# Flamingo block with two ternary and 8-bit-quantised products: the weights' magnitudes are summed in the first phase and their signs are taken by ScalarE

## The chip, the cores and the metric

The kernel runs on 1 core of one Trainium2 chip. The metric is the device time of one execution in microseconds (us), as the median of several runs. Engines: PE is TensorE (PEld its weight loads), DVE is VectorE, ACT is ScalarE, POOL is GpSimd, SP is SyncE, which here only issues DMAs.

## The reference

Inputs are `x` and a context, both 16 x 256 x 512 in float32, with weights. The result is `x` after four residual steps, each scaled by the tanh of a gate:

1. `x += tanh(g) * attention(layernorm(x), ctx)` with 16 heads, projections Wq, Wk, Wv, Wo and a strided mask;
2. `x += tanh(g) * experts(layernorm(x))`, where every expert picks one token of each group of 16 by a maximum of logits;
3. `x += tanh(g) * attention(layernorm(x), ctx)` without projections, with a mask;
4. `x += tanh(g) * ffn(layernorm(x))`, with

```
h   = layernorm(x) * ln_g + ln_b
h   = quant8(h) @ ternary(w1).T          w1: 2048 x 512
h   = gelu(h)                            exact
out = quant8(h) @ ternary(w2).T          w2: 512 x 2048

quant8(a):  amax = max(quantile(|a|, 0.995), 1e-5);  clip(round(a*127/amax), -128, 127)*amax/127
ternary(w): gamma = mean(|w|) + 1e-5;  clip(round(w/gamma), -1, 1)*gamma
```

So a ternary weight is gamma times -1, 0 or +1, and it is not 0 where |w| is over gamma/2. The kernel keeps the -1, 0 and +1 as bf16, transposed (`w1T`, `w2T`), and multiplies gamma in later.

## The kernel before

The program is a row of stages, each a block in which the five engines run their own instruction lists and meet at semaphores; a barrier of all engines ends a stage.

**phase1** (line 157) does residual step 1 and the logits of step 2. It works one batch entry (256 tokens) at a time, as a software pipeline of 18 steps: step b does F for entry b (turning the context and the normalised x by TensorE transposes, the k, v and q projections), M for entry b-1 (scores, softmax, attention, output projection) and T for entry b-2 (second layernorm, logits, selections). Steps 2 to 13 run as a loop of pairs, the others are written out; F, M and T are absent where there is no entry. Each engine's list of a step is written by hand in the function `step` of its block. What matters at the end of a step: TensorE does the output projection of entry b-1 into two PSUM banks (`rows_of("o", ...)`, line 344), VectorE adds each bank to the residual (line 791, semaphore `x1_done`), SyncE waits for `x1_done` and issues the write of that entry (line 316). SyncE's next step begins with the loads of x and ctx for the next entry (lines 278, 283). ScalarE's list of a step ends with a wait for TensorE's output projection and no work. What matters at the start of a step: TensorE turns the context of entry b (line 328), ScalarE copies it from PSUM as the high part `p_ctxTh` (line 503), VectorE subtracts to get the low part `p_ctxTl` (line 646), TensorE does the scores of entry b-1 (lines 378 to 387) and then turns the normalised x into the same two PSUM banks as the context, so it waits for `p_ctxTl` before it does.

**phase2a** and **phase2b3** do the experts and residual step 3, and leave the layernormed rows `hid` and the candidates `cand` (the 8 largest magnitudes of each stretch) for the first quantile.

**quantile1** (line 1675) finds the 0.995 quantile in 16 rounds of a radix-four search on the bits. In a round VectorE makes four trial values (line 1810), VectorE counts `cand` against two of them (line 1813), ScalarE against one (a Relu at 1744 and a Sign at 1746), TensorE sums the counts over the partitions (1763, the tile `q_tot`), and VectorE picks (1820, 1822). Beside it the ternary w1 is made: SyncE loads w1 and w2 whole (1706, 4 MB each); ScalarE sums magnitudes by an Abs with an accumulator, 2048 columns at a time, four for w1 in rounds 1 to 4 and four for w2 in rounds 6 to 9 (line 1726); gamma and the thresholds plus and minus gamma/2 (`th`, `nth`) come from line 1730 on; POOL compares each 128 x 2048 piece of w1 with `nth` and with `th` (1715, 1716), which gives two masks in bf16; TensorE turns both masks into one PSUM bank, the one by the identity and the other by minus the identity, so that the bank holds above minus below (`ternary_turn`, 1568); ScalarE evicts each bank of 128 x 512 into `w1T` (1739), two banks a round in rounds 8 to 15.

**quantise_hidden** and **product_tops** quantise `hid`, multiply by `w1T`, apply Gelu, and leave candidates again.

**quantile2** (line 2000) searches the second quantile in 17 rounds over whole numbers. In a round VectorE makes one trial (1620, 2097), ScalarE maps it by Gelu (2073) and counts 2304 columns of `cand` by a Sign (2075), VectorE counts the other 1792 (2100), TensorE sums (2053, 2055), VectorE decides (1624, 1627). Beside it `w2T` is made in the same way as `w1T`, a quarter of w2 at a time: SyncE loads 1 MB (2027), POOL makes two masks (2035, 2036), TensorE turns four banks, and ScalarE evicts them (2069), two at the end of each of two rounds.

**ffn** multiplies by `w2T` and adds to the output.

```
def phase1 ... def step(b, par, F, M, T, L):      # SyncE, the end of a step
    if M:
        sp.wait_ge(s["x1_done"], n.next(s["x1_done"], NT))
        n.apart()
        sp.dma_start(xm[b - 1], x1[1 - par][:, :, :]).then_inc(s["x1_out"], 16)
def phase1 ... def step(b, par, F, M, T, L):      # ScalarE, the start and the end
    if F:
        for t in range(NT):
            high(ctxT, t, "ctx_high")
    ...
    if M:
        act.wait_ge(s["M_full"], n.next(s["M_full"], NT))
```

Of the kernel before, what the change touches and what calls it, by code (L numbers as in the profile page):

```python
# [156 lines left out]
def phase1(nc, x, ctx, gx, Wq, bq, Wk, bk, Wv, bv, Wo, bo, ctrl, K, x_mid, xparts, perm_d, vg_d):  # L157
# [5 lines left out]
    with ExitStack() as es:  # L163
# [333 lines left out]
        def _(act):  # L497
# [1177 lines left out]
def quantile1(nc, cand, hid, K, amax, w1, w2, w1T, gam, th, nth):  # L1675
# [3 lines left out]
    ABS = {0: (1, 2, 3, 4), 1: (6, 7, 8, 9)}  # L1679
    SUM = {4: 0, 9: 1}  # L1680
    GAMMA = {5: 0, 10: 1}
    TURN = {8 + k: (2 * k, 2 * k + 1) for k in range(WQ * GQ // 2)}
    with ExitStack() as es:
        sw = es.enter_context(semaphores(nc, "qa_", [f"{q}_{n}" for q in ("q1", "q1s") for n in Search.NAMES] + """w_in0 w_in1 quads_in trial_ready
            above_done act_counted counted4 told4 step4 consts identb_done summed sums_full tsum_done gamma_done th_done signs_done turn_full turn_taken""".split()))
# [6 lines left out]
        W = [sbt(f"w{k}", [P, FC * D]) for k in range(2)]  # L1692
        sink, asum, tsum, eps = sbt("sink", [P, WC], BF16), sbt("asum", [P, 2 * WQ]), sbt("tsum", [P, 2]), sbt("eps", [P, 1])
        below_w, over_w = [[sbt(f"{n}{i}", [P, WC], BF16) for i in range(2)] for n in ("below", "above")]
        identb, minus = sbt("identb", [P, P], BF16), sbt("minus", [P, P], BF16)
# [5 lines left out]
        @block.sync  # L1701
        def _(sp):
            sp.dma_start(quads[:, :], K["c_quads"]).then_inc(sw["quads_in"], 16)
            fast.load(sp)
            for k, (w, rows) in enumerate(((w1, FC), (w2, C))):
                sp.dma_start(W[k][:, :].rearrange("p (c k) -> p c k", c=rows), w.rearrange("(c p) k -> p c k", p=P)).then_inc(sw[f"w_in{k}"], 16)
            slow.load(sp)

        @block.gpsimd
        def _(pool):  # L1710
            pool.wait_ge(sw["th_done"], 1)
            for k in range(WQ):
                if k >= 2:
                    pool.wait_ge(sw["turn_full"], GQ * (k - 1))
                pool.tensor_scalar(below_w[k % 2][:, :], W[0][:, k * WC:(k + 1) * WC], nth[:, 0:1], None, ALU.is_lt)
                pool.tensor_scalar(over_w[k % 2][:, :], W[0][:, k * WC:(k + 1) * WC], th[:, 0:1], None, ALU.is_gt).then_inc(sw["signs_done"], 1)

        @block.scalar
        def _(act):

# [16 lines left out]
            def turned(g):  # L1737
                act.wait_ge(sw["turn_full"], g + 1)
                act.activation(w1T[:, :, g * P:(g + 1) * P], bturn[g % 2][:, :].rearrange("p (c k) -> p c k", c=C), ACT.Copy).then_inc(sw["turn_taken"], 1)

            act.wait_ge(sw["consts"], 1)
            for r in range(ROUNDS):
# [5 lines left out]
                for w in range(2):  # L1748
                    if r in ABS[w]:
                        absolute(w, ABS[w].index(r))  # L1750
                if r in GAMMA:
                    thresholds(GAMMA[r])
                for g in TURN.get(r, ()):
                    turned(g)

        @block.tensor
        def _(pe):
            n = Count(pe)
            pe.wait_ge(sw["consts"], 1)
            for r in range(ROUNDS):  # L1760
# [3 lines left out]
                if r in SUM:  # L1764
                    w = SUM[r]
                    pe.wait_ge(sw["summed"], (w + 1) * WQ)
                    pe.matmul(bsum[:, w * WQ:(w + 1) * WQ], fast.ones[:, :], asum[:, w * WQ:(w + 1) * WQ], start=True, stop=True).then_inc(sw["sums_full"], 1)
# [694 lines left out]
```

## Time and profile before

| | us |
|---|---|
| median of 3 runs | 1668.54 (1667.11 to 1671.72) |
| the profiled execution, its own time | 1669.37 |
| its span in the trace | 1667.6 |
| TensorE busy | 1328.3 (80%) |
| VectorE busy | 1022.5 (61%) |
| ScalarE busy | 743.1 (45%) |
| POOL busy | 507.4 (30%) |

The span is 1.8 us shorter than the profiled execution's time, which has the launch around it. phase1 takes about the first third of the span, the first search runs from 1169.5 to 1252.3 us and the second from 1433.7 to 1533.4 us. In phase1 TensorE has nearly no idle time; in the two searches every engine has some, and a round is as long as the chain of waits from one trial to the next.

### The profile page before, as it was taken

Reading aid. Unit: us, or ns where it says so; the run is one execution under the profiler, and the core shown is the slowest. Engines: PE = TensorE matmul, PEld = TensorE weight load, DVE = VectorE, ACT = ScalarE, POOL = GpSimd, SP = SyncE. Lnnn points to the kernel's source line nnn. Section 1 sums busy time; section 2 is a strip of 40 time slices with the busy share of each in tenths; the row PEclk is TensorE's granted clock in tenths of the full one; section 3 lists DMA queues with packets and bytes.
Section 4 is the critical chain, followed back from the end, with each engine's and each line's share of the span. In section 5 each row is a group of like instructions: output and inputs, shape, how many; then the busy total and the mean of one; then the engine's idle time right before and its main releaser. Section 6 shows DMA issues by size and latency. Waiting matters only on the chain. (4 is left out here: it accounts for less than half of the span.)

```text
span 1667.6 us, 24905 instructions
## 1 busy us (share of the span) xinstructions
PE 1328.3 (80%) x8908; PEld 935.9 (56%) x8930; DVE 1022.5 (61%) x2344; ACT 743.1 (45%) x1113; POOL 507.4 (30%) x435
## 2 busy tenths in 40 slices
PE   5999999999999639999948999983143899133996
PEld 5887888788878437666415666653133444132443
DVE  5576667766675423444425878775566488745774
ACT  3233333333333113344414565552774555355991
POOL 1133333333333110000004787865180000253011
PEclk9999999999999769999979999996555899555998
DMA  6112221212211175565789788830500477211974
GB/s 212 46 65 72 85 100 66 70 69 101 80 65 46 65 271 193 224 244 216 276 275 287 235 233 232 236 96 25 207 1 3 173 305 304 77 47 35 413 311 154
DMA packets 105207, 259.18 MB, mean 155 GB/s; under 512 B 17456, under 2 KB 28816, under 8 KB 97424
## 3 DMA queue, kind: packets, MB, share of 16 engines
q1 hardware_dynamic: 95808, 232.59, 40.0%
q0 software_dynamic: 6384, 24.12, 3.9%
q10 hardware_dynamic: 2912, 1.14, 0.3%
q8 instruction: 59, 0.97, 0.3%
q14 instruction: 44, 0.36, 0.1%
HBM read 152.18 MB, written 105.64 MB: 155 GB/s over the span
## 5 line engine op out<-in xcount | busy, mean ns | idle before, releaser
L1191 PE MATMUL p_s<-p_rows,p_permT 128*128 128x512 f32 x256 | 132.0, 614 | 1.1 <-ACT p_permT L1284 1.1
L913 PEld LDWEIGHTS p_sel<-p_pick,p_xp 128*128 128x128 bf16 x1536 | 89.2, 100 | 57.5 <-issue 31.1
L913 PE MATMUL p_sel<-p_pick,p_xp 128*128 128x128 bf16 x1536 | 100.7, 223 | 23.8 <-DMA p_xp<-xparts 22.7
L2296 PE MATMUL p_o<-w2T,p_Gq 128*128 128x512 bf16 x501 | 111.7, 383 | 8.4 <-DVE p_Gq L2353 7.9
L1937 PE MATMUL p_z<-qT,w1T 128*128 128x512 bf16 x501 | 112.6, 385 | 3.0 <-PEq L113 2.5
L1043 DVE COPY p_selT<-p_sel 128x512 f32<-128x512 f32 x64 | 44.3, 692 | 99.8 <-PE p_sel L913 99.8
L2035 POOL TENSOR_SCALAR q_wbelow<-q_w,nth 128x2048 bf16<-128x2048 f32 x4 | 21.8, 5442 | 228.2 <-DMA q_w<-in_L_ffn_w_dram 192.6
L1996 DVE MAX8 cand<-hid 128x8 f32<-128x128 f32 x384 | 74.7, 296 | 25.3 <-ACT hid L1984 25.3
L2296 PEld LDWEIGHTS p_o<-w2T,p_Gq 128*128 128x128 bf16 x512 | 50.3, 99 | 69.4 <-DVE p_Gq L2353 8.1
L1937 PEld LDWEIGHTS p_z<-qT,w1T 128*128 128x128 bf16 x512 | 50.6, 99 | 64.8 <-issue 6.0
L990 ACT ACTIVATE p_selT<-p_sel 128x512 f32<-128x512 f32 x64 | 38.2, 598 | 91.8 <-PE p_sel L913 91.8
L344 PE MATMUL p_M<-p_ctxTh,p_Wkh 128*128 128x256 f32 x256 | 75.4, 295 | 1.9 <-DVE p_Wkl L668 1.9
L344 PE MATMUL p_M<-p_xnTh,p_Wqh 128*128 128x256 f32 x256 | 75.0, 293 | 1.1 <-DVE p_V L741 1.1
L2053 PE MATMUL q_tot<-q_signs,q_half 128*128 128x1 f32 x34 | 9.9, 362 | 79.3 <-ACT q_junk_a L2075 79.3
L344 PE MATMUL p_M<-p_ctxTh,p_Wkl 128*128 128x256 f32 x256 | 72.7, 284 | 0.0
L344 PE MATMUL p_M<-p_ctxTl,p_Wkh 128*128 128x256 f32 x256 | 72.7, 284 | 0.0
L344 PE MATMUL p_M<-p_xnTl,p_Wqh 128*128 128x256 f32 x256 | 72.0, 281 | 0.0
L344 PE MATMUL p_M<-p_xnTh,p_Wql 128*128 128x256 f32 x256 | 72.0, 281 | 0.0
L892 POOL DMA_DIRECT2D p_f<-in_L_ffn_f_dram x16 | 8.9, 556 | 201.0 <-PE p_in L930 195.2
L1763 PE MATMUL q_tot<-q_cnt,q_ones 128*128 128x4 f32 x32 | 9.3, 360 | 76.0 <-ACT q_junk_a L1746 40.2
L510 ACT ACTIVATE p_qT<-p_M,p_bqT 128x256 f32<-128x256 f32 x64 | 26.9, 471 | 95.4 <-PE p_M L344 95.4
L592 POOL TENSOR_TENSOR p_rs<-p_ve,p_mhalf 128x2 f32<-128x2 f32 x32 | 22.4, 699 | 154.0 <-DVE p_ve L658 153.9
(334 smaller groups left out, 4016.8 us busy)
## 6 DMA issues: line engine op xcount, KB each, us to landing
inter_d<-p_stage SPq DMA_DIRECT2D x64, 512.0 KB, 3.2
p_rows<-inter_d SPq DMA_DIRECT2D x128, 256.0 KB, 5.3
activations<-hid SPq DMA_DIRECT2D x24, 1024.0 KB, 3.9
p_cin<-in_ctx_dram SPq DMA_DIRECT2D x32, 512.0 KB, 5.1
xparts<-p_parts SPq DMA_DIRECT2D x16, 768.0 KB, 3.3
hid<-activations SPq DMA_DIRECT2D x10, 1024.0 KB, 8.9
p_xp<-xparts SPq DMA_DIRECT2D x3, 3072.0 KB, 25.2
p_xin<-in_x_dram SPq DMA_DIRECT2D x16, 512.0 KB, 4.1
```

What stands on the lines that cost most here:

```text
L344: mm = pe.matmul(out, left[a][:, c, lcols], right[e][:, c, rcols], start=(k == 0), stop=(k == len(terms) - 1))
L510: a = act.activation(dst[:, c, :], bM[k][:, (c % 2) * S:(c % 2 + 1) * S], ACT.Identity, bias=bias[:, c:c + 1])
L592: pool.tensor_tensor(out[:, :], var[:, :], mhalf[:, :], ALU.pow).then_inc(s[done], 1)
L913: mm = pe.matmul(bsel[u % 2][:, k * P:(k + 1) * P], xp[:, c, tile, r, :], pick[sb % 2][:, tile, :, :].rearrange("p s g -> p (s g)"), start ...
L990: act.activation(*picked(q, u), ACT.Copy).then_inc(s["sel_act"], 1)
L1043: dve.tensor_copy(*picked(q, u)).then_inc(s["sel_dve"], 1)
L1191: mm = pe.matmul(bo[t][:, :], permT[b % 2][:, t, k, :], R[b % 2][:, t, k, :], start=(k == 0), stop=(k == NK - 1))
L1937: mm = pe.matmul(bank, w1T[:, c, fc * P:(fc + 1) * P], qT[:, c, bass.ds(first, TB)], start=(c == 0), stop=(c == C - 1))
L1996: a = dve.max(cand[:, c:c + 8], Gs[j % R][:, :, k * OCT:(k + 1) * OCT])
L2035: pool.tensor_scalar(below_w[:, :], wc[:, :], nth[:, 1:2], None, ALU.is_lt)
L2053: pe.matmul(fast.tot[:, 0:1], half[:, :], signs[:, :], start=True, stop=False)
L2296: mm = pe.matmul(bo[i % 2][t][:, :], Gq[n % QR][:, k, t * P:(t + 1) * P], w2T[:, h * QUAD + k, :], start=(h == 0 and k == 0), stop=(h == N ...
```

## The change

The magnitudes of w1 and w2 are summed in phase1: in each of the 16 steps that have F, SyncE loads 256 KB of each matrix into `wabs` at the very end of its step, after the residual's write, and ScalarE takes an Abs with an accumulator of both at the very end of its step. `asum` (two tiles of 128 x 16) is carried to the first search, where the sums over partitions and both thresholds are made in round 0. w2 is no longer loaded in the first search.

POOL has no part in the searches any more. ScalarE takes two signs of each piece, sign(w - gamma/2) and sign(w + gamma/2), by a Sign with `nth` and with `th` as its bias: in the first search one in each of rounds 1 to 8, in the second in rounds 1, 2, 4, 5, 7, 8, 10 and 11. TensorE turns both by half the identity, so that a bank holds half the sum of the signs. VectorE evicts the banks in place of ScalarE, two in a round, between its count and its wait for TensorE's sum, and adds and subtracts MAGIC (3 * 2^22), which rounds to a whole number: rounds 4 to 11 of the first search, rounds 3, 4, 6, 7, 9, 10, 12 and 13 of the second.

```
@@ phase1 @@
+        wabs = sbt("wabs", [P, 2, D])
+        wv = [w.rearrange("a b -> (a b)").rearrange("(n p k) -> n p k", p=P, k=D) for w in (w1, w2)]
@@ phase1, SyncE, the end of step @@
                     sp.dma_start(xm[b - 1], x1[1 - par][:, :, :]).then_inc(s["x1_out"], 16)
+                if F:
+                    if (used := n.reuse(s["abs_done"])) is not None:
+                        sp.wait_ge(s["abs_done"], used)
+                        n.apart()
+                    for k in range(2):
+                        sp.dma_start(wabs[:, k, :], wv[k][b]).then_inc(s["abs_in"], 16)
@@ phase1, ScalarE, the end of step @@
                     act.wait_ge(s["M_full"], n.next(s["M_full"], NT))
+                if F:
+                    act.wait_ge(s["abs_in"], n.next(s["abs_in"], 32))
+                    for k in range(2):
+                        a = act.activation(wabs[:, k, :], wabs[:, k, :], ACT.Abs, accum_out=asum[k][:, bass.ds(b, 1)])
+                    a.then_inc(s["abs_done"], 1)
@@ ternary_turn @@
-        pe.matmul(bank[:, i * P:(i + 1) * P], over[:, cols], identb[:, :], start=True, stop=False)
-        mm = pe.matmul(bank[:, i * P:(i + 1) * P], below[:, cols], minus[:, :], start=False, stop=True)
+        for k in range(2):
+            mm = pe.matmul(bank[:, i * P:(i + 1) * P], signs[k][:, cols], halfid[:, :], start=(k == 0), stop=(k == 1))
@@ quantile1 @@
-    ABS = {0: (1, 2, 3, 4), 1: (6, 7, 8, 9)}
-    SUM = {4: 0, 9: 1}
-    GAMMA = {5: 0, 10: 1}
-    TURN = {8 + k: (2 * k, 2 * k + 1) for k in range(WQ * GQ // 2)}
+    SIGN = {1 + i: i for i in range(2 * WQ)}
+    TURN = {3 + 2 * k + i: (GQ * k + 2 * i, GQ * k + 2 * i + 1) for k in range(WQ) for i in range(2)}
...
-        def _(pool):
...
@@ quantile1, ScalarE @@
+            def sign(i):
+                c, k = divmod(i, 2)
+                if i == 0:
+                    act.wait_ge(sw["w_in"], 16)
+                    act.wait_ge(sw["th_done"], 2)
+                if c >= 2 and k == 0:
+                    act.wait_ge(sw["turn_full"], GQ * (c - 1))
+                act.activation(signs[c % 2][k][:, :], W[:, c * WC:(c + 1) * WC], ACT.Sign, bias=(nth, th)[k][:, 0:1]).then_inc(sw["signs_done"], 1)
...
+                if r == 0:
+                    act.wait_ge(sw["sums_full"], 1)
+                    for w in range(2):
+                        thresholds(w)
+                if r in SIGN:
+                    sign(SIGN[r])
@@ quantile1, VectorE, after the two counts of a round @@
+                for g in TURN.get(r - 1, ()):
+                    dve.wait_ge(sw["turn_full"], g + 1)
+                    dve.tensor_scalar(w1T[:, :, g * P:(g + 1) * P], bturn[g % 2][:, :].rearrange("p (c k) -> p c k", c=C), MAGIC, MAGIC, ALU.add, ALU.subtract).then_inc(sw["turn_taken"], 1)
@@ quantile2 @@
-    TURN = {4 + 3 * k + i: (GQ * k + 2 * i, GQ * k + 2 * i + 1) for k in range(WQ) for i in range(2)}
+    SIGN = {1 + 3 * c + k: (c, k) for c in range(WQ) for k in range(2)}
+    TURN = {2 + 3 * k + i: (GQ * k + 2 * i, GQ * k + 2 * i + 1) for k in range(WQ) for i in range(2)}
...
```

SyncE's list in phase1, from one step's end into the next step's start, inside the loop of pairs. `p_sharedk` holds the finished residual rows, `p_wabs` the new tile. Before:

```order
L316 ISA [waits p1_x1_done]
L316 DMA residual<-p_sharedk 128x2x512
L276 REGISTER_ALU [waits p1_norm1]
L278 ISA [waits p1_xb_done]
L278 DMA p_xin<-in_x_dram 128x2x512
L283 DMA p_cin<-in_ctx_dram 128x2x512 [waits p1_ctx_high]
```

and now:

```order
L318 ISA [waits p1_x1_done]
L318 DMA residual<-p_sharedk 128x2x512
L324 ISA [waits p1_abs_done]
L324 DMA p_wabs<-in_L_ffn_w_dram 128x512 x2
L278 REGISTER_ALU [waits p1_norm1]
L280 ISA [waits p1_xb_done]
L280 DMA p_xin<-in_x_dram 128x2x512
L285 DMA p_cin<-in_ctx_dram 128x2x512 [waits p1_ctx_high]
```

The two loads of a step stand behind the wait for `x1_done` of that step and ahead of the next step's loads.

ScalarE's list at the same place. Before:

```order
L579 ACTIVATE p_perm<-p_T 128x128 [waits p1_perm_out,p1_T_full]
L582 REGISTER_ALU
L502 REGISTER_ALU [waits p1_M_full]
L503 ACTIVATE p_ctxTh<-p_T 128x4x128 [waits p1_T_full]
L502 REGISTER_ALU
L503 ACTIVATE p_ctxTh<-p_T 128x4x128 [waits p1_T_full]
L528 REGISTER_ALU
L529 ACTIVATE p_sharedo<-p_S 128x512 [waits p1_S_full]
```

and now:

```order
L587 ACTIVATE p_perm<-p_T 128x128 [waits p1_perm_out,p1_T_full]
L590 REGISTER_ALU
L592 ISA [waits p1_M_full]
L594 ISA [waits p1_abs_in]
L594 ACTIVATE p_wabs,asum<-p_wabs 128x512
L594 REGISTER_ALU
L594 ACTIVATE p_wabs,asum<-p_wabs 128x512
L510 REGISTER_ALU
L511 ACTIVATE p_ctxTh<-p_T 128x4x128 [waits p1_T_full]
```

Between the wait for the output projection and the first copy of the next step there is now a wait for a DMA (`abs_in`) and two instructions.

VectorE's list in the first search, in a round from 4 to 11, now (before, the two rows of line 1817 were not there):

```order
L1807 TENSOR_TENSOR q_trial<-q_cur,q_quads 128x5 [waits p1_perm_done]
L1810 TENSOR_SCALAR q_junk,q_cnt<-cand,q_trial 128x1024 [waits p1_xnT]
L1810 TENSOR_SCALAR q_junk,q_cnt<-cand,q_trial 128x1024
L1817 TENSOR_SCALAR w1T<-q_turn 128x4x128 [waits p1_S_full] x2
L1819 SCALAR_TENSOR_TENSOR q_sel<-q_tot,q_trial 128x4 [waits p1_atT_global]
L1821 TENSOR_REDUCE q_cur<-q_sel 128x1 [waits p1_perm_done]
```

The two evictions stand ahead of the wait for TensorE's sum (semaphores are used again by later stages, so the names printed here are those of phase1).

## Rows read from the trace of the kernel before

**Rows 1.** Windows: span, busy us (instructions) of PE, PEld, DVE, ACT, POOL, clock, DMA, GB/s.

```profile
75.00:545.00 470.00, 468.49 (x3343) 385.24 (x3341) 320.33 (x693) 169.57 (x350) 163.75 (x97) 1.00 0.23 78
```

**Rows 2.** Timeline of TensorE (start, duration, instruction, count, [idle<-releaser]), start of two steps.

```profile
311.66 0.64 PE L378 MATMUL p_S<-p_qT,p_kbd 128*32 128x256 f32 x8
...
313.10 1.09 PE L328 MATMUL p_T<-p_ident,p_xn 128*128 128x128 f32 x8
...
345.33 0.64 PE L378 MATMUL p_S<-p_qT,p_kbd 128*32 128x256 f32 x8
```

**Rows 3.** Timeline of VectorE, the same step's start.

```profile
310.90 0.75 DVE L791 SCALAR_TENSOR_TENSOR p_sharedk<-p_M,p_tg,p_xb 128x512 f32<-128x512 f32 x1 [2.04 <-PE p_M L344]
...
311.96 1.29 DVE L646 TENSOR_TENSOR p_ctxTl<-p_T,p_ctxTh 128x512 fp32r<-128x512 f32 x2 [0.32 <-ACT p_ctxTh L503]
```

**Rows 4.** Timeline of ScalarE, the same step's start.

```profile
311.33 1.09 ACT L503 ACTIVATE p_ctxTh<-p_T 128x512 fp32r<-128x512 f32 x2 [5.36 <-PE p_T L328]
```

**Rows 5.** Timeline of SyncE's queue, the same step's start.

```profile
311.89 0.39 SPq L316 DMA_DIRECT2D residual<-p_sharedk  x1
...
312.70 0.41 SPq L278 DMA_DIRECT2D p_xin<-in_x_dram  x1
```

**Rows 6.** DMA issues: queue, count, KB each, median us from issue to landing.

```profile
p_xin<-in_x_dram SPq DMA_DIRECT2D x1, 512.0 KB, 4.0
...
out_dram<-p_y SPq DMA_DIRECT2D x4, 256.0 KB, 2.1
```

**Rows 7.** Step 1's start: timeline of TensorE, then a window (columns as rows 1).

```profile
43.37 1.08 PE L378 MATMUL p_S<-p_qT,p_kbd 128*32 128x256 f32 x8 [4.34 <-DVE p_qbd L781]
...
43.30:47.70 4.40, 4.33 (x32) 2.58 (x33) 2.21 (x6) 1.06 (x2) 0.00 (x0) 0.50 0.00 0
```

**Rows 8.** Groups by line, ScalarE: count, busy us, mean ns, idle before.

```profile
L1726 ACT ACTIVATION_READ_ACCUMULATOR q_sink<-q_w 128x1 f32 x8 | 1.5, 188 | 0.0
```

**Rows 9.** Timeline of ScalarE, start of step 16.

```profile
547.68 0.60 ACT L529 ACTIVATE p_sharedo<-p_S 128x512 f32<-128x512 f32 x1 [6.02 <-PE p_S L380]
```

**Rows 10.** First search: timeline of VectorE, then of ScalarE.

```profile
1173.35 0.17 DVE L1810 TENSOR_TENSOR q_trial<-q_cur,q_quads 128x5 int32<-128x5 int32 x1
...
1176.78 0.16 DVE L1820 SCALAR_TENSOR_TENSOR q_sel<-q_tot,q_trial 128x4 f32<-128x4 f32 x1 [0.74 <-PE q_tot L1763]
...
1177.16 0.17 DVE L1810 TENSOR_TENSOR q_trial<-q_cur,q_quads 128x5 int32<-128x5 int32 x1
...
1188.09 0.17 DVE L1810 TENSOR_TENSOR q_trial<-q_cur,q_quads 128x5 int32<-128x5 int32 x1
...
1192.35 0.17 DVE L1810 TENSOR_TENSOR q_trial<-q_cur,q_quads 128x5 int32<-128x5 int32 x1
...
1252.26 0.15 DVE L1647 COPY q_above<-q_cur 128x1 f32<-128x1 f32 x1
...
1182.80 1.91 ACT L1726 ACTIVATE q_sink<-q_w 128x2048 bf16<-128x2048 f32 x1 [6.85 <-DMA q_w<-in_L_ffn_w_dram]
```

**Rows 11.** Second search: timeline of VectorE, of ScalarE, then two groups by line.

```profile
1438.41 2.26 DVE L1620 TENSOR_TENSOR q_trial<-q_cur,q_bits 128x1 f32<-128x1 f32 x1
...
1450.62 0.16 DVE L1620 TENSOR_TENSOR q_trial<-q_cur,q_bits 128x1 f32<-128x1 f32 x1
...
1454.75 0.16 DVE L1624 TENSOR_SCALAR q_keep<-q_tot 128x1 int32<-128x1 f32 x1 [1.19 <-PE q_tot L2055]
...
1455.31 0.16 DVE L1620 TENSOR_TENSOR q_trial<-q_cur,q_bits 128x1 f32<-128x1 f32 x1
...
1533.41 0.15 DVE L2103 TENSOR_SCALAR q_below<-q_cur 128x1 f32<-128x1 f32 x1
...
1455.69 0.30 ACT L2073 ACTIVATE q_at<-q_below,zs 128x1 f32<-128x1 f32 x1 [2.05 <-DVE q_below L2097]
...
L2315 ACT ACTIVATE cand<-hid,p_below 128x2048 bf16<-128x2048 f32 x18 | 35.9, 1996 | 0.6
...
L2035 POOL TENSOR_SCALAR q_wbelow<-q_w,nth 128x2048 bf16<-128x2048 f32 x4 | 21.8, 5442 | 228.2 <-DMA q_w<-in_L_ffn_w_dram 192.6
```

More of the change, by code:

```diff
@@ L154, in shape_constants, with phase1 @@
     }
-def phase1(nc, x, ctx, gx, Wq, bq, Wk, bk, Wv, bv, Wo, bo, ctrl, K, x_mid, xparts, perm_d, vg_d):
+def phase1(nc, x, ctx, gx, Wq, bq, Wk, bk, Wv, bv, Wo, bo, ctrl, K, x_mid, xparts, perm_d, vg_d, w1, w2, asum):
     xt = x.rearrange("b (t p) d -> b p t d", p=P)
@@ L1691, in quantile1 @@
         cnt4, sel4 = sbt("cnt4", [P, WAYS - 1]), sbt("sel4", [P, WAYS - 1])
[L1692 to L1695, printed above, removed]
+        W = sbt("w", [P, FC * D])
+        sink, tsum, eps = sbt("sink", [P, B], BF16), sbt("tsum", [P, 2]), sbt("eps", [P, 1])
+        signs = [[sbt(f"signs{i}{k}", [P, WC], BF16) for k in range(2)] for i in range(2)]
+        halfid = sbt("halfid", [P, P], BF16)
         ps = lambda n: es.enter_context(nc.psum_tensor("q1_" + n, [P, 512], F32))
@@ L1763, in _ @@
                 pe.matmul(tot4[:, 0:WAYS - 1], fast.ones[:, :], cnt4[:, :], start=True, stop=True).then_inc(sw["told4"], 1)
[L1764 to L1767, printed above, removed]
+                if r == 0:
+                    for w in range(2):
+                        mm = pe.matmul(bsum[:, w * B:(w + 1) * B], fast.ones[:, :], asum[w][:, :], start=True, stop=True)
+                    mm.then_inc(sw["sums_full"], 1)
                 for g in TURN.get(r, ()):
@@ L2064, in _, with sign @@
             n = Count(act)
-            def turned(g):
-                act.wait_ge(s["turn_full"], g + 1)
-                k, f = divmod(g, GQ)
-                act.activation(w2T[:, f * C:(f + 1) * C, k * P:(k + 1) * P], bturn[g % 2][:, :].rearrange("p (f k) -> p f k", f=C), ACT.Copy).then_inc(s["turn_taken"], 1)
+            def sign(c, k):
+                if k == 0:
+                    act.wait_ge(s["w_in"], 16 * (c + 1))
+                    if c:
+                        act.wait_ge(s["turn_full"], GQ * c)
+                act.activation(wsigns[k][:, :], wc[:, :], ACT.Sign, bias=(nth, th)[k][:, 1:2]).then_inc(s["signs_done"], 1)
             def step(i):
@@ L2075, in step @@
                 act.activation(junk_a[:, :], cand[:, 0:NA], ACT.Sign, bias=at[:, :], scale=-1.0, accum_out=signs[:, :]).then_inc(s["signed"], 1)
-                for g in TURN.get(i, ()):
-                    turned(g)
+                if i in SIGN:
+                    sign(*SIGN[i])
             for i in range(IBITS):
@@ L2416, in mk_flamingo_gated @@
     g_d = dram("activations", (P, NB, FC, TB))
-    phase1(nc, x, ctx, gx, Wq, bq, Wk, bk, Wv, bv, Wo, bo, ctrl, K, x_one, xparts, perm_d, vg_d)
-    phase2a(nc, xparts, perm_d, f1, bias, f2, K, inter_d)
     with ExitStack() as es:
         sbt = lambda n, s, d=F32: es.enter_context(nc.sbuf_tensor(n, s, d))
+        asum = [sbt(f"asum{k}", [P, B]) for k in range(2)]
+        phase1(nc, x, ctx, gx, Wq, bq, Wk, bk, Wv, bv, Wo, bo, ctrl, K, x_one, xparts, perm_d, vg_d, w1, w2, asum)
+        phase2a(nc, xparts, perm_d, f1, bias, f2, K, inter_d)
         cand = sbt("cand1", [P, NC1])
```

78 lines of the change are left out of this document (24 added, 54 removed).

## The prediction

> **What bounds the kernel now.** I read three places: the boundary between two steps of phase1, since new work is put there, and the two searches, which the rest of the change is about.
>
> In phase1 the windows show TensorE busy for 468.49 of 470.00 us at a granted clock of 1.00 [rows 1]. A step takes 345.33 - 311.66 = 33.7 us by the scores of two entries in a row [rows 2], and there is no idle time of TensorE that a delay could be taken from: whatever holds TensorE there lengthens the program. At the boundary the engines hang together closely. VectorE finishes `x1_done` at 310.90 + 0.75 = 311.65 [rows 3], SyncE issues the residual's write at 311.89 and the next load at 312.70 [rows 5], and meanwhile ScalarE has started the high part of the context at 311.33 [rows 4], VectorE the low part at 311.96 [rows 3], and TensorE the second set of transposes at 313.10 [rows 2]. ScalarE's 5.36 us of idle time in front of 311.33 look like room for more work. They end with the last moment at which it is needed.
>
> In the searches the round is the chain. In the first, an undisturbed round takes 1177.16 - 1173.35 = 3.81 us; one in which ScalarE also has an Abs of 2048 columns takes 1192.35 - 1188.09 = 4.26; the 13 rounds from round 3 to the end take 1252.26 - 1188.09 = 64.17, so 14.6 over 13 x 3.81 [rows 10]. In the second, an undisturbed round takes 1455.31 - 1450.62 = 4.69, and the 16 rounds from round 1 take 1533.41 - 1438.41 = 95.00, so 20.0 over 16 x 4.69 = 75.0 [rows 11]. Part of this excess is ScalarE waiting for turned banks that it has to evict. Part is a VectorE instruction on one element that lasts 2.26 us in place of 0.16, while POOL is at masks of 5.44 us each [rows 11].
>
> **Phase1, the new work.** ScalarE's list now has, ahead of the context's high part, a wait for the two loads of this same step, and SyncE issues them only behind this step's `x1_done`. So the loads can't be early. Their issue: the residual's at 311.89 as before, then the first at about 312.6 and the second at about 313.2 (the next load stood at 312.70 with 0.41 us of issue, rows 5). Their landing: together they are 512 KB behind the residual's 512 KB, exactly what the load of x was, which landed 4.0 us after 312.70, at 316.7 [rows 5, 6]. Then two Abs with accumulator: 0.55 us each from start to start (1.09 for two of 512 columns, rows 4) and 0.19 for each accumulator [rows 8], so 1.5. The context's high part starts at about 318.2 in place of 311.33: ScalarE is 6.9 us late. VectorE's low part was 0.4 us ahead of TensorE's need: its first half (of 1.29 for two) ended at 312.6, TensorE took it at 313.10 [rows 2, 3]. TensorE's work in between (scores, from 311.66, rows 2) needs none of this and is done by then. So TensorE stands for 6.5 us.
>
> It then restarts at the lower clock. At step 1's start TensorE had stood 4.34 us; the window behind it shows a granted clock of 0.50 (1.2 GHz) over 4.40 us, and the windows are back at about full rate behind 47.70 [rows 7]. Half of 4.4 is 2.2 us lost for work that fills it, as it does here.
>
> How often: the wait bites at the end of steps 1 to 15. At the end of step 0 SyncE has no `x1_done` to wait for, the loads go out in the middle of the step, and TensorE waits for VectorE until 43.37 in any case [rows 7]; nothing. Fourteen boundaries lead into a full step: 14 x (6.5 + 2.2) = 121.8. The last leads into step 16, where ScalarE's first work is the copy of the scores at 547.68 [rows 9], 0.3 us behind that step's `x1_done`; ScalarE is free 6.5 us behind it, so 6.2, and TensorE has little to do there, so I add 0.8 for the clock: 7.0. **Sum of phase1: +129 us.** The two DMA issues also stand ahead of SyncE's loads of x and ctx, 1.2 us. They are needed in the middle of the step and at the next step's start, while x lands 4.0 us after its issue [rows 6], so this costs nothing; if the stall went, nothing would be late in its place. The 8 MB of loads are small against the 78 GB/s that phase1 moves [rows 1].
>
> For the landing, the bounds are 2.1 us from the second issue (a 256 KB transfer with nothing ahead of it, rows 6) and about 1 us more than taken; for the clock, nothing and 3.4 us a stall, one and a half times the row's. The Trainium skill has a price for this, in "DMA: Bandwidth & Descriptors", section "Anatomy of one DMA": about 2.0 us plus the bytes over 436 GB/s, so an estimate of 2.6 us for 256 KB, measured there on GpSimd's path. By it alone the second load would land at 315.8, and the sum would be 15 x 0.9 = 13 us smaller; the row of the load of x, with the write ahead of it, says otherwise, and I follow the row.
>
> **First search.** w2's load and all eight Abs go; w1's stays, and ScalarE's first sign waits for it in round 1 just as its first Abs did (idle 6.85 us until 1182.80, rows 10). The thresholds now stand in round 0, about 2.3 us on ScalarE, but they are covered by that same wait. So round 3 starts at 1188.09 as before. It has a sign in place of an Abs: the row of a Sign of 2048 columns with a pointer bias says 1.996 [rows 11], against 1.91 [rows 10] plus an accumulator; the same within 0.1, so 4.26. Rounds 4 to 11 have two evictions on VectorE. Its idle time before the pick is 0.74 in an undisturbed round [rows 10], two reads of a PSUM bank take 1.29 [rows 3], so 3.81 - 0.74 + 1.29, and 0.04 for the handover: 4.4. This is over ScalarE's 4.26, so VectorE sets these rounds, and the signs are covered. Rounds 12 to 15 are undisturbed. Sum 4.26 + 8 x 4.4 + 4 x 3.81 = 54.7, against 64.2: **-9.5 us**. Without a gain in the evictions (0.1 each) it would be -8, and if w1 lands sooner with w2 off the queue, up to 1.6 better. TensorE's turns come behind its sum in a round, as before, and have half a round.
>
> **Second search.** ScalarE idles 2.05 us before each Gelu [rows 11]; a sign of 1.996 us, which starts when the count's accumulator is read, just fits: nothing, or 0.1 in 8 rounds. VectorE idles 1.19 before its decision [rows 11] and has evictions of 1.29 there in 8 rounds: 8 x 0.15 = 1.2. w2's next quarter is asked for at the start of a round and needed a round and a half later, 7 us; 1 MB at the rate at which 512 KB behind 512 KB took 4.0 + 0.8 us [rows 5, 6] needs less. 75.0 + 1.2 = 76.2 against 95.0: **-18.8 us**. The covers are thin; if both failed by 0.3 us this would be -14.
>
> **The sum:** 129 - 9.5 - 18.8 = +100.7 us on the profiled execution's 1669.4, so 1770. The median shown is 0.8 us lower, and I give 1769.
>
> **The rivals.**
> *The loads don't queue behind the write.* Then they land 2.1 us after the second issue [rows 6], at 315.3, 1.4 us sooner, 15 x 1.4 = 21 less: 1748. For it: the page above. Against: the load of x.
> *The clock does not fall.* 15 stalls without the 2.2: 33 less, 1737. Against: TensorE fell after 4.34 us [rows 7].
> *The searches gain nothing*, because the signs and evictions take the place of what they remove: 1669.4 + 129 = 1798. For it: both covers in the second search are within 0.2 us. Against: POOL's masks, on which rounds hung, are gone.
> *The other side, the new wait is covered.* ScalarE's 5.36 us of idle time [rows 4] take both Abs, phase1 keeps its length, and 28 us are gained: 1641, faster. It decides at one point: the loads must have landed 1.5 us before the high part is due, less 0.4, so by 310.2. The issue behind `x1_done` is at 312.6, so this needs the order of SyncE's list to be other than it is written, or TensorE to have slack that [rows 1] doesn't show.
>
> **How the numbers follow.** Chances: my forecast 0.62, the loads sooner 0.12, no fall of the clock 0.08, no gain in the searches 0.10, the wait covered 0.04, and 0.04 for something not seen here. The range goes from 1735 to 1800. Its low end takes in the clock that doesn't fall (1737) and, inside it, the early landing (1748). Its high end takes in searches without a gain (1798), or landings 1 us later (15 us more) together with half of the clock's upper bound. What is left out is both low cases at once, the covered wait and what I haven't seen, about 1 in 10. A measurement of this kernel can tell about 0.3%, 5 us, from no change. All but the covered wait lie far above that: faster 0.04, same 0.01, slower 0.95.
>
> **What would show it.** In phase1 a step of 42.4 us in place of 33.7; ScalarE idle before `p_wabs` until a DMA, some 5 us after `x1_done`; TensorE idle 6.5 us before the transposes of `p_xn`, and a granted clock of 0.5 for some 4 us behind it. In the first search rounds 4 to 11 at 4.4 us; in the second all rounds between 4.7 and 4.9, and no one-element instruction of VectorE over 0.4 us. Steps of 33.7 us would make the forecast wrong as a whole; steps of 40 us its clock term; a `p_wabs` landing by 315.5 its landing.

## Result, and the profile after

The change makes the kernel slower: 1755.3 us median (1752.04 to 1759.24) against 1667.82 us on the same chip, a ratio of 1.0523 with an interval of 1.0492 to 1.0554. The profiled execution has a span of 1752.0 us against 1667.6, 84.4 us more. The forecast was 1769 us, with a range from 1735 to 1800.

Busy us, share of the span and instructions of each engine, the first part of the page; POOL has lost its masks (507.4 us before), and TensorE is busy for longer in a longer span:

```profile
PE 1356.1 (77%) x8930; PEld 962.2 (55%) x8930; DVE 1036.9 (59%) x2374; ACT 759.4 (43%) x1145; POOL 421.2 (24%) x419
```

The next view is the window of phase1 that answers to [rows 1], over the same stretch, and two short ones behind two boundaries (span, busy us and count of PE, PEld, DVE, ACT and POOL, granted clock, share of the DMA engines, GB/s):

```profile
75.00:545.00 470.00, 394.72 (x2671) 327.37 (x2670) 260.22 (x554) 149.39 (x326) 130.79 (x78) 0.92 0.23 80
334.93:339.26 4.33, 4.33 (x21) 4.33 (x22) 2.83 (x6) 1.40 (x3) 0.00 (x0) 0.50 0.03 13
377.10:380.20 3.10, 3.10 (x15) 3.10 (x16) 2.61 (x6) 1.39 (x3) 0.00 (x0) 0.50 0.07 27
```

TensorE was busy for 468.5 us of these 470 and is now busy for 394.7, at a mean clock of 0.92 in place of 1.00. Right behind the two stalls it is at 0.50, which is 1.2 GHz. Its timeline at two boundaries in a row, to be read against [rows 2]:

```profile
327.48 0.64 PE L386 MATMUL p_S<-p_qT,p_kbd 128*32 128x256 f32 x8
...
334.93 1.97 PE L336 MATMUL p_T<-p_ident,p_xn 128*128 128x128 f32 x8 [5.95 <-DVE p_ctxTl L659]
...
369.12 0.64 PE L386 MATMUL p_S<-p_qT,p_kbd 128*32 128x256 f32 x8
...
377.10 1.97 PE L336 MATMUL p_T<-p_ident,p_xn 128*128 128x128 f32 x8 [6.47 <-DVE p_ctxTl L659]
```

This step takes 369.12 - 327.48 = 41.64 us against 33.67 (over the 14 full steps 41.0 to 42.9). Between the scores and the transposes of `p_xn`, 1.44 us apart before, there are now 7.45 and 7.98, and the transposes take 1.97 us in place of 1.09. Who is late stands in the lists of VectorE, SyncE and ScalarE at the second boundary, one fence each, against [rows 3 to 5]:

```profile
368.36 0.75 DVE L804 SCALAR_TENSOR_TENSOR p_sharedk<-p_M,p_tg,p_xb 128x512 f32<-128x512 f32 x1 [2.04 <-PE p_M L352]
```

```profile
369.35 0.39 SPq L318 DMA_DIRECT2D residual<-p_sharedk  x1
369.99 1.14 SPq L324 DMA_DIRECT2D p_wabs<-in_L_ffn_w_dram  x2
371.54 0.38 SPq L280 DMA_DIRECT2D p_xin<-in_x_dram  x1
```

```profile
374.50 0.63 ACT L594 ACTIVATE p_wabs<-p_wabs 128x512 f32<-128x512 f32 x1 [11.07 <-DMA p_wabs<-in_L_ffn_w_dram]
375.04 0.19 ACT L594 ACTIVATION_READ_ACCUMULATOR p_wabs<-p_wabs  x1
375.13 0.61 ACT L594 ACTIVATE p_wabs<-p_wabs 128x512 f32<-128x512 f32 x1
375.65 0.18 ACT L594 ACTIVATION_READ_ACCUMULATOR p_wabs<-p_wabs  x1
375.74 0.57 ACT L511 ACTIVATE p_ctxTh<-p_T 128x512 fp32r<-128x512 f32 x1
```

`x1_done` falls at 368.36 + 0.75 = 369.11. The loads go out at 369.99, ScalarE idles until they have landed, at 374.50, and the context's high part starts at 375.74, 6.63 us behind `x1_done`; before it started 0.3 us ahead of it. The page's groups by line have the same for all of phase1, 19.9 us of work behind 162.3 us of idle time:

```profile
L594 ACT ACTIVATE p_wabs<-p_wabs 128x512 f32<-128x512 f32 x32 | 19.9, 621 | 162.3 <-DMA p_wabs<-in_L_ffn_w_dram 162.3
```

In the searches the timeline of VectorE shows the rounds. First search: the first trial, the starts of rounds 3, 4 and 10, and the end, against [rows 10]:

```profile
1285.44 0.17 DVE L1807 TENSOR_TENSOR q_trial<-q_cur,q_quads 128x5 int32<-128x5 int32 x1 [1.30 <-DMA q_quads<-in_c_quads_dram]
...
1304.63 0.17 DVE L1807 TENSOR_TENSOR q_trial<-q_cur,q_quads 128x5 int32<-128x5 int32 x1
...
1308.89 0.17 DVE L1807 TENSOR_TENSOR q_trial<-q_cur,q_quads 128x5 int32<-128x5 int32 x1
...
1334.42 0.17 DVE L1807 TENSOR_TENSOR q_trial<-q_cur,q_quads 128x5 int32<-128x5 int32 x1
...
1358.07 0.15 DVE L1660 COPY q_above<-q_cur 128x1 f32<-128x1 f32 x1
```

Second search, against [rows 11]:

```profile
1543.35 0.16 DVE L1633 TENSOR_TENSOR q_trial<-q_cur,q_bits 128x1 f32<-128x1 f32 x1
1548.03 0.16 DVE L1633 TENSOR_TENSOR q_trial<-q_cur,q_bits 128x1 f32<-128x1 f32 x1
...
1618.27 0.15 DVE L2100 TENSOR_SCALAR q_below<-q_cur 128x1 f32<-128x1 f32 x1
```

Rounds 3 to 15 of the first take 53.44 us in place of 64.17, and the 16 rounds of the second 74.92 in place of 95.00, 4.68 each: the undisturbed round, every time.

The same marks divide every trace. The columns are the time from the scores of step 1 to those of step 16, from there to the first trial, the whole first search, the whole second search from its first trial (99.74 = 4.74 + 95.00 before), and the span:

| us | steps 1 to 16 | to the first trial | first search | second search | span |
|---|---|---|---|---|---|
| before | 503.1 | 623.0 | 82.7 | 99.7 | 1667.6 |
| the change | 616.8 | 624.4 | 72.6 | 79.7 | 1752.0 |
| loads early | 513.5 | 623.4 | 72.9 | 79.7 | 1648.5 |
| loads early, Abs ahead | 503.5 | 622.7 | 73.1 | 79.6 | 1639.8 |
| Abs a step later | 502.7 | 621.4 | 72.9 | 79.6 | 1634.0 |
| loads ahead of the write | 605.1 | 623.8 | 72.5 | 79.7 | 1739.2 |
| filled stall | 593.6 | 629.6 | 72.9 | 79.7 | 1735.4 |
| masks stay on POOL | 502.5 | 622.9 | 83.3 | 87.4 | 1657.1 |
| signs shifted | 503.2 | 624.8 | 66.9 | 79.7 | 1635.2 |
| signs shifted, thresholds split | 502.2 | 621.0 | 65.2 | 79.6 | 1627.6 |

The second column holds the end of phase1 and the phases between it and the search, which no kernel here touches; over the kernels without a stall in phase1 it scatters from 621.0 to 624.8. (The kernel with the filled stall stands out with 629.6, which I haven't followed up.) So +113.7 us lie in phase1's boundaries, +0.9 in front of step 1, +1.4 in the second column, -10.1 and -20.1 in the searches, and the remaining -1.4 around the searches: +84.4.

The 113.7 can be divided in the change's own trace. From the scores to the transposes of `p_xn` it takes 87.6 us more than before over all boundaries: the stalls, 6.26 at each of the 14. From there to the next scores it takes 26.0 us more, 1.9 at each: the work done at the low clock.

### The profile page after: what moved, and what is told of

Its sections match the earlier page's. It is cut to its first block and busy times, and to the rows that moved or that the text cites. A ratio compares the mean times of both kernels' runs of the same rounds, so it can differ in the third digit from the quotient of the medians.

```text
span 1752.0 us, 25073 instructions
## 1 busy us (share of the span) xinstructions
PE 1356.1 (77%) x8930; PEld 962.2 (55%) x8930; DVE 1036.9 (59%) x2374; ACT 759.4 (43%) x1145; POOL 421.2 (24%) x419
## 5 line engine op out<-in xcount | busy, mean ns | idle before, releaser
L2269 POOL DMA_DIRECT2D p_y<-residual x8 | 11.0, 1379 | 402.1 <-POOLq L113 341.5
L336 PE MATMUL p_T<-p_ident,p_xn 128*128 128x128 f32 x128 | 31.3, 426 | 91.8 <-DVE p_ctxTl L659 91.8
L594 ACT ACTIVATE p_wabs<-p_wabs 128x512 f32<-128x512 f32 x32 | 19.9, 621 | 162.3 <-DMA p_wabs<-in_L_ffn_w_dram 162.3
L352 PE MATMUL p_M<-p_ctxTh,p_Wkh 128*128 128x256 f32 x256 | 83.8, 327 | 1.9 <-DVE p_Wkl L681 1.9
L659 DVE TENSOR_TENSOR p_ctxTl<-p_T,p_ctxTh 128x512 fp32r<-128x512 f32 x32 | 20.6, 686 | 101.3 <-ACT p_ctxTh L511 101.3
L336 PEld LDWEIGHTS p_T<-p_ident,p_xn 128*128 128x128 f32 x128 | 25.1, 223 | 99.6 <-DVE p_ctxTl L659 66.7
L352 PE MATMUL p_M<-p_ctxTl,p_Wkh 128*128 128x256 f32 x256 | 79.6, 311 | 0.0
L352 PE MATMUL p_M<-p_ctxTh,p_Wkl 128*128 128x256 f32 x256 | 79.0, 309 | 0.0
```

The costliest lines, as they stand in the source:

```text
L336: return pe.transpose(dst, src, (idt if idt is not None else ident)[0:src.shape[0], 0:src.shape[0]])
L352: mm = pe.matmul(out, left[a][:, c, lcols], right[e][:, c, rcols], start=(k == 0), stop=(k == len(terms) - 1))
L594: a = act.activation(wabs[:, k, :], wabs[:, k, :], ACT.Abs, accum_out=asum[k][:, bass.ds(b, 1)])
L659: dve.tensor_tensor(dst[1][:, :, cols], bT[t][:, :].rearrange("p (c k) -> p c k", c=C), dst[0][:, :, cols].bitcast(F32), ALU.subtract).the ...
```

## Experiments

Ratios are to the kernel before on the same chip, with their intervals.

### Loads at the head of the step

```diff
 def step(b, par, F, M, T, L):          # SyncE
     if L: load(b + 1, 1 - par)
+    if F: <wait abs_done, two loads into wabs>
...
-    if F: <wait abs_done, two loads into wabs>
```

> The changed kernel with SyncE's two loads of the magnitudes moved to the head of the step, right behind the load of the next x and ctx; the two Abs stay where they are, behind the wait for the output rows. Theory (the late landing behind x1_done is what costs): the loads have some 28 us, the wait for them is gone, and only the Abs themselves remain in front of the context's high part. They took 1.24 us for two, and VectorE's low part has 0.4 us of slack before TensorE needs it, so up to 0.8 us at each of 15 boundaries, up to 12 us, and no fall of the clock: 1755 - 116 = 1639 for all of phase1's loss given back, 1640 to 1651 with the Abs in the way. Rival (the traffic or SyncE's two further issues cost): over 1700, with the steps still near 41 us.

Measured: 1649.88 us (0.9865, 0.9838 to 0.9892). The loads are issued a step's length ahead, and steps 2 to 14 take 34.2 to 34.4 us. This is the top of the expected 1640 to 1651. What is left is the Abs in front of the high part; timeline of ScalarE, then of TensorE:

```profile
351.58 0.63 ACT L594 ACTIVATE p_wabs<-p_wabs 128x512 f32<-128x512 f32 x1 [5.10 <-PE p_M L352]
...
352.82 1.06 ACT L511 ACTIVATE p_ctxTh<-p_T 128x512 fp32r<-128x512 f32 x2
```

```profile
354.18 1.26 PE L336 MATMUL p_T<-p_ident,p_xn 128*128 128x128 f32 x8 [0.50 <-DVE p_ctxTl L659]
```

ScalarE now idles until the output rows (`p_M`) and no longer until a DMA, and 5.10 us of that idle time are still unused, because the two Abs stand behind it.

### The Abs ahead of the wait for the output rows

```diff
-    if M: act.wait_ge(M_full, ...)
     if F: <wait abs_in, two Abs>
+    if M: act.wait_ge(M_full, ...)
```

> As the run before, and the two Abs stand ahead of ScalarE's wait for the output rows, in the 5.4 us in which it idles there. Theory: nothing is left in front of the context's high part, steps of 33.6 us as before the change, 1755 - 116 = 1639, up to 12 us less than the run before. Rival (accumulating Abs on ScalarE delays something in mid-step): more than the run before.

Measured: 1638.72 us (0.9808, 0.9791 to 0.9824). The same kernel was run once more, on another chip:

> The kernel with early loads and the Abs ahead once more, on the chip of these runs, as the one to compare with: 1637 to 1640, and the version with shifted signs and split thresholds 8 us below it.

Measured: 1639.55 us (0.9809, 0.9786 to 0.9831). Steps are back at 33.66 us and all of phase1's loss is gone. ScalarE's timeline shows both Abs in the room that was there; 4.14 us of it remain:

```profile
340.39 0.64 ACT L592 ACTIVATE p_wabs<-p_wabs 128x512 f32<-128x512 f32 x1
...
341.01 0.64 ACT L592 ACTIVATE p_wabs<-p_wabs 128x512 f32<-128x512 f32 x1
341.53 0.21 ACT L592 ACTIVATION_READ_ACCUMULATOR p_wabs<-p_wabs  x1
345.87 1.09 ACT L511 ACTIVATE p_ctxTh<-p_T 128x512 fp32r<-128x512 f32 x2 [4.14 <-PE p_T L336]
```

### The same loads as in the change, the Abs a step later

```diff
+    if M: <wait abs_in, two Abs into column b - 1>
     if M: act.wait_ge(M_full, ...)
-    if F: <wait abs_in, two Abs into column b>
```

> The changed kernel with the loads where they are, issued behind x1_done, but the Abs of step b's part moved to the end of step b + 1, ahead of ScalarE's wait for the output rows. Theory (only ScalarE's wait for the landing costs, not the transfers at this place): 1639, within 4 us of the run with early loads and the Abs ahead. Rival (two more issues and 512 KB at the boundary delay the loads of x and ctx or the residual): 15 x 1.2 us = 18 more, 1657 or over.

Measured: 1637.24 us (0.9805, 0.9788 to 0.9821). The loads leave at the very place where they leave in the change, land as late (3.5 us, the same median) and cost nothing, since nobody waits. So it is ScalarE's wait, and neither the 8 MB nor SyncE's further issues.

### The loads ahead of the residual's write

```diff
     sp.wait_ge(x1_done, ...)
+    <wait abs_done, two loads into wabs>
     sp.dma_start(xm[b - 1], x1[...])
-    <wait abs_done, two loads into wabs>
```

> The changed kernel with SyncE's order at the boundary turned: behind x1_done first the two loads of the magnitudes, then the residual's write. Theory (as in the prediction, the loads' data queue behind the 512 KB of the write): both the issue (0.6 us) and the queueing fall away, the last landing comes 1.4 to 2.0 us sooner at 15 boundaries, 21 to 30 us less: 1725 to 1734. Rival (a fixed latency from the issue, the write costs only its issue): 0.6 us sooner, 9 less: 1746.

Measured: 1744.52 us (1.0449, 1.0432 to 1.0467), 11 us less than the change by medians, 12 by the ratios: between the two expectations and nearer to the fixed latency. The groups of DMA issues (KB each, median us to landing), of the change and then of this kernel:

```profile
p_wabs<-in_L_ffn_w_dram SPq DMA_DIRECT2D x32, 256.0 KB, 3.5
residual<-p_sharedk SPq DMA_DIRECT2D x16, 512.0 KB, 3.1
```

```profile
p_wabs<-in_L_ffn_w_dram SPq DMA_DIRECT2D x32, 256.0 KB, 2.8
residual<-p_sharedk SPq DMA_DIRECT2D x16, 512.0 KB, 4.3
```

The write ahead costs the loads 0.7 us of landing beside the 0.6 of its issue, not the 1.4 that I had for the data alone. ScalarE's wait falls from 162.3 to 143.6 us, 1.2 us a boundary. TensorE gets less of it: its steps shorten by 0.8. Divided as above, the stalls fall from 87.6 to 70.8 us, and the work behind them loses 31.2 us to the clock in place of 26.0. One stretch at 1.2 GHz of this kernel, behind a stall of 4.72 us:

```profile
368.50:373.90 5.40, 5.37 (x25) 5.38 (x26) 2.86 (x6) 1.41 (x3) 0.00 (x0) 0.50 0.35 134
```

Read the same way, by the spacing of the matmuls, its 14 stretches last 3.0 to 5.4 us, 4.8 in the mean; the change's last 2.8 to 5.8, 4.1 in the mean. So the shorter stalls of this kernel are followed by somewhat more time at 1.2 GHz. Why is not shown: within the change the length of a stretch doesn't follow the length of its stall, as two of its boundaries below show.

### The stall filled with matmuls

```diff
     mm.then_inc(R_full, 1)
+    if F and M and not second:
+        pe.wait_ge(*n.mark("M0"))
+        for k in range(44):
+            pe.matmul(bM[0][:, 0:S], W["k"][0][:, 0, 0:P], W["k"][0][:, 1, 0:S], start=True, stop=True)
```

> The changed kernel with 44 matmuls of 256 columns added on TensorE behind the scores of the next entry, at the 14 boundaries from step 2 on: their product goes to the bank of the first key columns and is written over there. At 0.118 us each they take 5.2 us of the 6.0 to 6.5 us for which TensorE stands. Theory (each stall costs its length and 2.1 us for the low clock behind it): the granted clock stays at 1.00, the transposes of p_xn take 1.1 us in place of 1.97, and 14 x 2.1 = 29 us come back: 1726. Rival (the low clock behind the stall costs nothing that isn't covered): 1755.

Measured: 1734.59 us (1.0370, 1.0351 to 1.0389), 20.7 us less than the change by medians and about 26 by the ratios. Timeline and window:

```profile
358.46 5.53 PE L401 MATMUL p_M<-p_Wkh 128*128 128x256 f32 x44
364.49 1.25 PE L336 MATMUL p_T<-p_ident,p_xn 128*128 128x128 f32 x8 [0.50 <-DVE p_ctxTl L663]
```

```profile
364.40:368.80 4.40, 4.31 (x36) 4.13 (x37) 2.74 (x7) 1.62 (x4) 0.00 (x0) 1.00 0.05 17
```

Here the second column of the table takes back 5 us, so the steps are the better measure. The clock stays at 1.00, ScalarE waits as long as before (163.0 us), and steps 1 to 16 take 593.6 us. So 616.8 - 593.6 = 23.2 us of phase1's loss came back with the clock, 1.7 at each of 14 boundaries. The fill itself costs a little: from the scores to the transposes this kernel needs 1.5 us more than the change in sum, and the work behind them 1.4 more than the kernel before. That is the difference to the 26.0 us above. The expected 29 was too much.

### The searches alone

```diff
-    <both loads and both Abs of phase1>
+    act.activation(asum[k][:, :], stage["k"][:, k, 0:B], ACT.Abs)      # k = 0, 1, in step 0
```

> The changed searches alone: phase1 neither loads nor sums the magnitudes, and the thresholds are made from 16 columns of another weight, so the output is another. Theory: by the traces the two searches gained 10.1 and 20.1 us, and 1.3 lie around them: 1668 - 31 = 1637. With the run that has early loads and the Abs ahead this gives the price of the sums when they are covered: within 3 us by theory. Rival (part of the gain is an effect of the trace's alignment): 1645 or more.

This one lasted 19638 us and says nothing, as the next expectation tells.

```diff
-    <both loads and both Abs of phase1>
+    dve.memset(asum[0][:, :], 18.055808460183403)
+    dve.memset(asum[1][:, :], 9.030400654645415)
```

> Again the changed searches alone, since with thresholds of another size the kernel took its slow path for all values and lasted 19638 us, which says nothing on the question. Phase1 neither loads nor sums the magnitudes; the sums are set to constants of the size of the true ones, so the thresholds are not computed from w1 and w2. Theory: 1668 - 31 = 1637, and within 3 us of the run with early loads and the Abs ahead. Rival: 1645 or more.

Measured: 1639.03 us (0.9806, 0.9780 to 0.9832), beside 1639.55 for the kernel that does sum them, on the same chip. So the searches are worth 31 us, and the sums cost nothing once they are covered.

### The masks stay on POOL, only the evictions move

```diff
-    act.activation(w1T[...], bturn[g % 2], ACT.Copy)
+    dve.tensor_scalar(w1T[...], bturn[g % 2], MAGIC, MAGIC, ALU.add, ALU.subtract)    # a round later, both searches
```

> The kernel before with one part of the change: POOL still makes both masks, but VectorE evicts the turned banks, a round later, in both searches. Theory A (ScalarE's place in the chain was the cost, it waited for the banks before the next Gelu or count): rounds 11 to 15 of the first search fall from 5.22 to about 4.2, 6 us, and the second search loses most of its long rounds, 15 or more: 1647 or less. Theory B (POOL's cycle of two masks of 5.44 us and a load is the bound; whoever evicts waits for it): the first search gains 5, the second keeps its period of 18.95 us per quarter, gains under 5: 1658 to 1664.

Measured: 1657.91 us (0.9923, 0.9903 to 0.9944). The first search takes 83.3 us against 82.7, no gain at all, and the second 87.4 against 99.7. Neither theory holds as a whole: both gave the first search a gain of 5 or 6 us, and the second gained 12.4, over B's 5 and under A's 15. That the total of 1657.91 lies next to B's range is the sum of two misses. POOL's masks and VectorE's rounds in the first search:

```profile
1222.76 5.45 POOL L1715 TENSOR_SCALAR q_below<-q_w,nth 128x2048 bf16<-128x2048 f32 x1
1228.19 5.45 POOL L1716 TENSOR_SCALAR q_above<-q_w,th 128x2048 bf16<-128x2048 f32 x1
```

```profile
1225.09 1.41 DVE L1808 TENSOR_TENSOR q_trial<-q_cur,q_quads 128x5 int32<-128x5 int32 x1
...
1230.52 1.41 DVE L1808 TENSOR_TENSOR q_trial<-q_cur,q_quads 128x5 int32<-128x5 int32 x1
```

Rounds 10 to 14 last exactly one mask each, 5.43 us, and the five-element trials of rounds 11 to 15 take 1.41 us in place of 0.17. Each of these trials ends 3.74 us after a mask's start (1226.50 - 1222.76 and 1231.93 - 1228.19), in the middle of the mask. The round would take 4.18 us by the changed kernel's rounds with evictions alone, and 4.18 + 1.24 = 5.42. So the evictions' gain (5.22 to about 4.2 a round) is eaten by a wait of VectorE; none of the kernels without POOL's masks has it. In the second search the evictions alone give 12.4 of the 20.1 us, and the remaining 7.7 go with the masks. Signs on ScalarE with the evictions left there were not run.

### Two steps further

In the change, w1 lands 13.9 us behind the first trial, and the first sign, in round 1, holds the search until then: rounds 0 to 2 take 19.2 us.

```diff
-    SIGN = {1 + i: i for i in range(2 * WQ)}
-    TURN = {3 + 2 * k + i: ...}
+    SIGN = {4 + i: i for i in range(2 * WQ)}
+    TURN = {6 + 2 * k + i: ...}
```

> The version that the traces point to: loads at the head of the step, the Abs ahead of the wait for the output rows, and in the first search the signs begin in round 4 in place of 1, the turns in round 6 in place of 3. w1 lands 13.9 us after the first trial, and ScalarE's first sign, in round 1, held round 2 until then: the first three rounds took 19.2 us in place of 11.5. With the signs in rounds 4 to 11 nothing waits for the landing: 7.7 us less than the run without this shift, 1639 - 7.7 = 1631. Rival (w1's load is slowed or the wait moves to another place): 1639.

Measured: 1632.94 us (0.9770, 0.9757 to 0.9783). The first search takes 66.9 us, 6.2 less and not 7.7: round 1 still lasted 5.57 us, since both thresholds stood in front of its count. The wait for w1 had hidden them.

```diff
-    if r == 0:
-        act.wait_ge(sums_full, 1)
-        for w in range(2): thresholds(w)
+    if r in (1, 2):
+        if r == 1: act.wait_ge(sums_full, 1)
+        thresholds(r - 1)
```

> The version with shifted signs, and the thresholds of w1 in round 1 and those of w2 in round 2 in place of both in round 0, where they stood behind TensorE's sums and held round 1 for 5.57 us in place of 3.82. Theory: one pair takes 0.85 us and ScalarE has 1.33 us of idle time in a round, so rounds 1 and 2 take 3.82: 1.75 us less than the version before it, 8 us less than the run with the early loads alone. Rival (the chain of five short instructions holds each of the two rounds by some tenths): 1 us less.

Measured: 1630.53 us (0.9761, 0.9739 to 0.9783), 9.0 us less than the kernel without either edit beside it (8 were expected), and 2.4% under the kernel before. Rounds 0 to 4 all take 3.82 us, and the first search 65.2, the expected 1.75 less than with the signs shifted alone.

## Why the prediction was right, and where its terms were off

**Where the loss arises: right.** The loads behind `x1_done`, the wait ahead of the context's high part, and TensorE behind VectorE's low part all stand in the trace as forecast. Two kernels take the wait away, one with the loads early, one with the loads left where they are, and both get everything back.

**The wait: right within some tenths.** "ScalarE is 6.9 us late" was made of a landing 5.05 us behind `x1_done`, two Abs of 1.5, and the 0.3 us by which the high part had started ahead of `x1_done`. Measured at two boundaries in a row: a landing after 4.88 and 5.39, and 1.24 for the Abs, so 6.4 and 6.95. TensorE stands 5.95 and 6.47 us there where the forecast had 6.5; over all 14 boundaries the stalls cost 87.6 us against 14 x 6.5 = 91.0. The rival of loads that don't queue behind the write (1748) fell closest to the time, but by luck and not by its mechanism: the loads land 3.5 us after their issue and not 2.1. With no write ahead of them they take 2.8. The Trainium skill's "DMA: Bandwidth & Descriptors", section "Anatomy of one DMA", gives an estimate of 2.6 us for this size, from a fit on GpSimd's path. The traces agree within 0.2 for the loads of SyncE with no write ahead and are 0.9 over it behind a write. The row of 2.1 us that I took for a lower bound was a write, and no load here is that quick in the median.

**The clock behind a stall: too high.** I took "half of 4.4 is 2.2 us lost" from a stall of 4.34 us and put it behind stalls of 6.5. Measured: 1.9 a boundary, 26.0 us against 30.8 (23.2 by the filled kernel). The mean stretch at the low clock is 4.1 us and not 4.4, and what it costs is a little less than half of it. No one row could have given the size: it isn't set by the length of the stall. Here are two stalls of the change, with the window behind each, 2.84 us at 0.50 behind 5.91 and 5.57 behind 6.66; in others of its boundaries it is 5.57 behind 5.96 and 2.83 behind 6.40.

```profile
251.05 1.97 PE L336 MATMUL p_T<-p_ident,p_xn 128*128 128x128 f32 x8 [5.91 <-DVE p_ctxTl L659]
292.76 1.97 PE L336 MATMUL p_T<-p_ident,p_xn 128*128 128x128 f32 x8 [6.66 <-DVE p_ctxTl L659]
```

```profile
251.05:253.89 2.84, 2.84 (x14) 2.84 (x15) 2.35 (x6) 1.40 (x3) 0.00 (x0) 0.50 0.05 18
292.76:298.33 5.57, 5.57 (x26) 5.57 (x27) 2.83 (x6) 1.40 (x3) 0.00 (x0) 0.50 0.03 10
```

The rival without any fall of the clock (1737) is refuted by the windows at 0.50 and by the filled kernel.

**Step 16: 7.0 forecast, 1.4 found; the largest miss.** The scores' copy was indeed late, 668.05 - 661.00 = 7.05 us behind the scores in place of 1.19, so 5.9, and TensorE's output projection begins 6.2 us late (688.69 - 661.00 against 567.97 - 546.49). But VectorE's first output of the projection that ends the step starts at 691.86, 30.9 us behind the scores, against 27.1 before: only 3.8 us late, since that projection ran at a higher clock than it had before. The prediction had no term for this. Windows over it, of the change and of before:

```profile
688.50:694.50 6.00, 5.81 (x24) 4.43 (x24) 0.89 (x2) 0.00 (x0) 2.14 (x1) 1.00 0.35 137
```

```profile
567.70:576.30 8.60, 8.33 (x24) 6.35 (x24) 0.96 (x2) 0.04 (x1) 2.14 (x1) 0.66 0.24 95
```

I had added 0.8 for the clock there; it gave 2.4 back. What the stretch behind it adds, about -2, is within its scatter, so the 1.4 is known to some 2 us at best.

**The boundary of step 0: "nothing"** was 0.9 us. The scores of step 1 stand at 44.24 in place of 43.37. It is one boundary, and the kernels without a stall show 43.9 to 44.7 too.

**The searches: right, a little low.** First, -9.5 forecast from round 3 on and -10.7 measured: rounds 4.25 us, not 4.4. "VectorE sets these rounds" was the wrong engine. As long as a sign is in the round ScalarE sets it (2.00 + 1.13 + 1.06 + 0.19, less their overlap), and the two rounds with evictions alone take 4.19. w1's load set round 3's start, as forecast, but the first trial now stands 0.5 us behind the load's issue in place of 1.2, so the three rounds in front take 0.6 us more. Second, -18.8 forecast and -20.1 measured: both covers held, so the 0.15 us in 8 rounds did not come. What I had not separated was POOL's share, and the kernel with POOL's masks shows it: while they stay, the moved evictions gain nothing in the first search.

**The sum.** Against the forecast of +100.7 the span moved by +84.4: of the 16.3 between, 5.6 are step 16, 4.8 the clock, 3.4 the stalls, 1.9 the searches, and 1.4 lie around the searches, and step 0 takes 0.9 back (16.2 by these roundings). Nearly all terms were too high, so the sum was not helped by errors that cancel. The other side's rival (1641, if the wait is covered) did not happen but was priced well: covered, the kernel takes 1639.

## What to carry to other kernels

Work that fits an engine's idle time must also have its data there when that time begins: ask which event ends the idle time and which event the new load hangs on, and if it is the same one, the full latency lands on the path, here 116 us for 20 us of work. The cure was an order of two lists, no faster instruction. And a wait that is removed uncovers what it had hidden, as the thresholds behind w1's landing: look again after each step.

## What the runs showed of the hardware

- TensorE's time at 1.2 GHz behind a stall is not a fixed price, and the stall's length doesn't give it: 2.84 us behind 5.91, 5.57 behind 6.66, 5.57 behind 5.96 and 2.83 behind 6.40, in one kernel. Shortening the stalls by 1.2 us each shortened the steps by 0.8. Matmuls of no use, put in the stall, kept the granted clock at 1.00 and made the kernel 21 us faster.
- A two-input instruction of VectorE on five elements takes 1.41 us in place of 0.17 in five rounds while POOL runs a mask of 5.44 us, and the rounds fall into step with the masks. It ends 3.74 us after the mask's start. So does the longest one in the kernel before (1.78 us, begun at 1219.12, beside a mask begun at 1217.16), where with the same masks the instruction takes from 0.17 to 1.78 us, by where in the mask it falls. The Trainium skill's "GPSIMD Engine Reference", section "Specifications", says that GpSimd shares its SBUF interfaces with VectorE and contends with instructions that have two SBUF inputs; the trace agrees, 1.24 us each time in the kernel with the moved evictions, and VectorE's one-input counts between them kept their 1.28 us.
- In the median a load of 256 KB issued behind a 512 KB write of the same queue lands 3.5 us after its issue, ahead of it 2.8; the write lands after 3.1 and 4.3. The order shifts 0.7 us to the one and 1.2 to the other.
